# Two Flamingo layers on one core: the gate's rounding under the up projection, and weight splits put off behind the routing

## The chip, the cores and the metric

The kernel runs on one core of a Trainium2 chip. A core has TensorE (PE) for matrix products, VectorE (DVE), ScalarE (ACT), GpSimd (POOL) and SyncE (SP); each works through its own queue of instructions in order and waits on semaphores for the others. The metric is the device time of one execution in microseconds (us). The kernel before took 1800.84 us, the median of 3 runs (1798.96 to 1802.85).

## The reference

The input x has 16 sequences of 112 tokens (1792 tokens in all) and 256 features. Four residual blocks follow each other; `g` are learned gates.

```
x = x + tanh(g_xattn[0]) * attention_0(layernorm(x), ctx)      # 16 heads of 64, context of 375
x = x + tanh(g_ffn[0])   * feed_forward_0(layernorm(x))        # quantised, 256 -> 768 -> 256
x = x + tanh(g_xattn[1]) * attention_1(layernorm(x), ctx)      # 16 heads of 16
x = x + tanh(g_ffn[1])   * mixture(layernorm(x))               # shared expert + top 2 of 8, 256 -> 1024 -> 256
```

The two blocks that matter here are

```
# feed_forward_0; q(v) = clip(round(v / s), -32768, 32767) * s with s = max|v| / 32767 over the whole tensor
x = q(x); up = q(x @ W_up.T); gate = q(x @ W_gate.T)
sig = clip(round(sigmoid(gate) * 65536), 0, 65535) / 65536
gate = q(gate * sig); o = q(gate * up); return o @ W_down.T
# mixture
shared = relu(normed @ sw1 + sb1) @ sw2 + sb2
probs = sigmoid(flat @ router_w.T); scores, idx = top_k(probs, 2); w = scores / (sum(scores) + 1e-6)
routed = sum over the two experts of w * (relu(flat @ ew1 + eb1) @ ew2 + eb2)
```

Each `q` needs the largest absolute value of a whole tensor before any of it can be rounded. With a scale s, rounding is a multiplication by 1/s and a round to the nearest integer.

## The kernel before

The program is a sequence of phases, each a block with a barrier of all engines at its end: a setup, attention 0, a normalisation with the quantisation of the weights, `feed_forward0_phase` (L631), attention 1, the mixture's front `moe_front_phase` (L1312) and `routed_experts_phase` (L1864). Products in near-float32 precision are three float16 matmuls each (high by high, low by high, high by low, L291 to L293), so every operand is split: ACT rounds it to float16 (the high part) and DVE subtracts that from the value (the low part).

**Feed-forward 0.** The 1792 tokens are four groups (`NG`) of 448 columns (`GW`); the 768 hidden features are six slices (`OC0`) of 128. A job is one slice of one group of one projection. PE does, group by group, the six up jobs and then the six gate jobs, into six PSUM slots. ACT copies each job to `U` or `G` (L710), and DVE reduces six of them to their largest absolute value (L774). After the last group, POOL's all-reduce (L742) spreads the maximum over the partitions and DVE makes the scales (L787 to L795). Then six slices of 1792 columns pass through a pipeline. ACT rounds the gate by adding the constant MAGIC (L714), DVE subtracts it again (L798), ACT takes the sigmoid (L699) and rounds it in the same way (L701, L754), DVE multiplies (L755) and reduces (L757). POOL rounds U meanwhile (L747). The result's maximum gives the next scale (to L805), ACT rounds again (L722, L726), DVE multiplies gate and up (L809) and reduces (L812). The last maximum gives the output scale and the gate of the residual (to L819). The output is rounded and split in four groups of 2688 columns (six slices of 448: L731 and L734 on ACT, L823 on DVE), each released to PE as a whole. PE does one token row `t` of 16 after another (18 matmuls each), DVE adds each to the residual (L763).

**The mixture's front.** It does the shared expert for all tokens, decides the routing, and prepares the weights of all nine experts. The shared expert runs in 32 steps: four groups of four rows, eight slices of 128 hidden features each. In step `n` PE computes the slice's up projection (into `m_p1`, printed `m_p`), ACT applies bias and relu (L1604) and rounds to float16 (L1608), DVE subtracts (`low(n)`, L1667), and three steps later (`LAG`) PE multiplies into `m_p2` (L1560). After a group's last slice `add(g)`, four DVE operations on L1674, moves `m_p2` to `y`; only then can PE begin the next group's second products, and POOL adds `y` to the output in memory (L1461). `add(g)` waits for the store of the group before, since there is one `y`.

Between these stand two other streams. 36 weight chunks of 512 KB come by DMA into three stage buffers (SP, L1433), and each is split by ACT (L1592) and DVE (L1655); SP refills a buffer when DVE has split what it held. The table `CHUNKS` gives the step in which a chunk is split. The routing is a long run of small DVE operations that ends in masks: three of 1120 columns for the tiles (L1818 first, then L1822) and two of 2048 columns for the rows (L1825). PE multiplies them in step `FIND_AT` (the find, L1530), DVE makes row indices, and POOL gathers the first token tiles (L1457). Then POOL makes the bias of each tile of tokens (L1465, L1470).

The order of all work inside an engine is the order in which the code issues it; there is no planner. The lines that decide when PE goes on at a group's edge are

```
def add(g):
    dve.wait_ge(down_done, g * HC1 + HC1)
    wait(dve, stored, 16 * g)
    for i in range(TG):
        nc.vector.tensor_scalar(y[:, i, :], p2[0:S, i, 0:D], gate[:], None, ALU.mult).then_inc(added, 1)
```

## Time and profile before

| | |
|---|---|
| median of 3 runs | 1800.84 us (1798.96 to 1802.85) |
| profiled execution | 1801.27 us |
| its span | 1799.5 us |
| granted clock of TensorE, mean | 0.897 |
| PE busy | 1422.7 us (79%) |
| DVE busy | 1245.4 us (69%) |
| ACT busy | 1138.1 us (63%) |
| POOL busy | 244.2 us (14%) |

The span runs from the first to the last instruction of one profiled execution; the execution's time is 1.8 us longer. Busy shares are means over phases with different limits. In the profile PE's "clock" is the granted share of full speed. A row of a timeline gives an instruction's start in us from the span's start, its length, engine, line and operation, what it writes and reads with the shapes, how many such follow each other (x4), and in brackets the idle time before it with what ended that. Names there have lost their numbers: `f0_G` is `f_G`, and `m_p1` and `m_p2` are both `m_p`. What the program calls `x_res` in the front is the large tensor `x_all`, in which masks and gathered tiles lie too.

### The profile page before, as it was taken

The numbers are of one execution on the slowest core, as the hardware profiler recorded it, in microseconds if no ns is written. First come the engines' busy times: TensorE is split into PE (matmuls) and PEld (weight loads), VectorE is DVE, ScalarE is ACT, GpSimd is POOL, SyncE is SP. The second block draws the span as 40 slices with busy tenths as digits, with TensorE's granted clock in tenths as the row PEclk, the third lists the DMA queues.
The fourth block names the chain that finished last, engine by engine and source line by source line (L and its number), as shares of the span: only waits on it lengthen the run. The fifth ranks groups of instructions, "written<-read, shape, count | busy, mean of one in ns | idle before, by whom it ended". The sixth has DMA issues, their size and how long they took to land. (4 is left out here: it accounts for less than half of the span.)

```text
span 1799.5 us, 40814 instructions
## 1 busy us (share of the span) xinstructions
PE 1422.7 (79%) x15436; PEld 1013.3 (56%) x15436; DVE 1245.4 (69%) x3030; ACT 1138.1 (63%) x2422; POOL 244.2 (14%) x202
## 2 busy tenths in 40 slices
PE   1799999999999954900738889898898476779996
PEld 1566676766766643500725666666665354558885
DVE  6567777777677777478447889888887676534443
ACT  5466666666666633465436888888887444546664
POOL 4400001000010013020050000000000004024443
PEclk9999999999999986955857999999998687879998
DMA  4110000100010010000010001011000424522222
GB/s 145 35 36 19 19 19 19 36 19 19 19 27 18 2 54 1 0 0 0 10 42 22 24 25 31 17 31 32 17 26 4 127 64 130 175 42 44 46 46 28
DMA packets 36652, 66.09 MB, mean 37 GB/s; under 512 B 5161, under 2 KB 25618, under 8 KB 36466
## 3 DMA queue, kind: packets, MB, share of 16 engines
q1 hardware_dynamic: 27890, 53.40, 9.7%
q0 software_dynamic: 8576, 10.10, 3.6%
q8 instruction: 129, 2.11, 0.5%
q14 instruction: 57, 0.47, 0.1%
HBM read 48.16 MB, written 16.24 MB: 36 GB/s over the span
## 5 line engine op out<-in xcount | busy, mean ns | idle before, releaser
L519 ACT ACTIVATE a_pt<-a_ps_t 125x336 f16<-125x336 f32 x256 | 102.6, 448 | 107.5 <-PE a_ps_t L450 107.2
L1180 ACT ACTIVATE a_p<-a_s,a_nb 112x375 f32<-112x375 f32 x256 | 140.9, 598 | 26.9 <-DVE a_nb L1281 26.0
L291 PE MATMUL a_ps_o<-a_vh,a_pt 125*128 125x64 f16 (+1 forms) x1536 | 153.2, 183 | 3.0 <-ACT a_pt L1193 0.8
L293 PE MATMUL a_ps_o<-a_vh,a_pt 125*128 125x64 f16 (+1 forms) x1536 | 151.3, 182 | 0.0
L292 PE MATMUL a_ps_o<-a_vl,a_pt 125*128 125x64 f16 (+1 forms) x1536 | 151.2, 182 | 0.0
L1105 PE MATMUL a_ps_t<-ident,a_p 112*128 112x112 f32 x768 | 119.4, 287 | 39.8 <-ACT a_p L1180 39.3
L511 ACT ACTIVATE a_p<-a_ps_s,a_nb 112x375 f32<-112x375 f32 x256 | 144.1, 573 | 3.0 <-DVE a_scaled L591 3.0
L291 PEld LDWEIGHTS a_ps_o<-a_vh,a_pt 125*128 125x128 f16 x1536 | 133.8, 98 | 15.7 <-ACT a_pt L1193 7.5
L292 PEld LDWEIGHTS a_ps_o<-a_vl,a_pt 125*128 125x128 f16 x1536 | 131.2, 98 | 11.2
L1272 DVE TENSOR_TENSOR a_s<-a_ps_s,a_mask 112x750 f32<-112x750 f32 x128 | 119.8, 936 | 25.4 <-PE a_ps_s L1095 20.4
L1105 PEld LDWEIGHTS a_ps_t<-ident,a_p 112*128 112x128 f32 x768 | 81.2, 148 | 95.1 <-issue 80.2
L1281 DVE CUSTOM_DVE_ANT_0 a_s<-a_s,a_fill 112x375 f32<-112x375 f32 x256 | 130.0, 546 | 5.5
L591 DVE TENSOR_SCALAR_CACHE_REDUCE a_scaled<-a_ps_s 112x375 f32<-112x375 f32 x256 | 129.0, 541 | 5.1 <-POOL x_res L544 3.9
L572 DVE TENSOR_TENSOR a_vl<-a_ps_j,a_vh 125x512 f16<-125x512 f32 x96 | 66.4, 692 | 93.2 <-ACT a_vh L495 93.2
L1966 ACT ACTIVATE e_h<-e_p,tile_b 128x128 f32<-128x128 f32 x280 | 86.8, 368 | 68.6 <-PE e_p L293 65.6
L293 PEld LDWEIGHTS a_ps_o<-a_vh,a_pt 125*128 125x128 f16 x1536 | 129.4, 97 | 0.0
L1998 DVE TENSOR_TENSOR e_hl<-e_h,e_hh 128x512 f16<-128x512 f32 x70 | 48.5, 692 | 101.8 <-ACT e_hh L1973 101.8
L597 DVE TENSOR_TENSOR a_pt<-a_ps_t,a_pt 125x336 f16<-125x336 f32 x256 | 116.9, 498 | 1.1 <-ACT a_pt L519 1.0
L291 PE MATMUL a_ps_j<-a_cx,a_wk 128*128 128x375 f16 x320 | 106.2, 332 | 14.0 <-POOL a_neg L1217 10.4
L291 PE MATMUL a_ps_j<-a_wv,a_cx 128*125 128x512 f16 (+1 forms) x384 | 111.2, 308 | 2.6 <-DVE a_kl L1233 1.3
L291 PE MATMUL e_p<-e_xth,w1h 128*128 128x128 f16 x560 | 110.3, 222 | 1.6 <-DVE e_xtl L1992 1.6
L292 PE MATMUL e_p<-e_xtl,w1h 128*128 128x128 f16 x560 | 110.2, 222 | 0.0
(366 smaller groups left out, 4656.4 us busy)
## 6 DMA issues: line engine op xcount, KB each, us to landing
m_stage<-in_w SPq DMA_DIRECT2D x36, 512.0 KB, 4.2
a_ctx<-in_ctxT SPq DMA_DIRECT2D x16, 375.0 KB, 3.6
ctx<-a_cx SPq DMA_DIRECT2D x16, 375.0 KB, 4.3
a_cx<-ctx SPq DMA_DIRECT2D x16, 375.0 KB, 3.7
a_mask<-in_mask SPq DMA_DIRECT2D x16, 164.1 KB, 2.3
x_res<-in_x SPq DMA_DIRECT2D x1, 1792.0 KB, 9.5
out_x<-x_res SPq DMA_DIRECT2D x16, 112.0 KB, 2.2
normed_rows<-x_res SPq DMA_DIRECT2D x4, 448.0 KB, 5.1
```

The lines of the kernel that those rows point to most:

```text
L291: nc.tensor.matmul(out, wh, mh, start=(i == 0), stop=False)
L292: nc.tensor.matmul(out, wh, ml, start=False, stop=False)
L293: last = nc.tensor.matmul(out, wl, mh, start=False, stop=(i == n - 1))
L511: nc.scalar.activation(p32[:, g % 2, i, 0:NC], ps_s[0:S, i, 0:NC], ACT.Exp, bias=nb[:, g % 2, i:i + 1], scale=SC, accum_out=rsum[:, h:h + ...
L519: nc.scalar.activation(pt[:, g % 2, i, 0, :, 0:S], ps_t[0:KV, i, 0:NKV * S].rearrange("p (t s) -> p t s", t=NKV), ACT.Copy).then_inc(pt_hi, 1)
L591: nc.vector.tensor_scalar(scaled[:, i, :], ps_s[0:S, i, 0:NC], -SC, None, ALU.mult, ALU.min, accum_out=nb[:, g % 2, i:i + 1]).then_inc(max ...
L597: nc.vector.tensor_tensor(pt[:, g % 2, i, 1, :, 0:S], ps_t[0:KV, i, 0:NKV * S].rearrange("p (t s) -> p t s", t=NKV), pt[:, g % 2, i, 0, :, ...
L1105: mm = nc.tensor.matmul(ps_t[:, 2 * (g % 2) + i, t * S:(t + 1) * S], p32[:, g % 2, i, t * KV:t * KV + 128], ident32[0:S, 0:S], start=(t == ...
L1180: nc.scalar.activation(p32[:, g % 2, i, 0:NC], s2[:, g % 2, i, :], ACT.Exp, bias=nb[:, g % 2, i:i + 1], scale=-1.0).then_inc(exp_done, 1)
L1272: nc.vector.tensor_tensor(s1[:, r], ps_s[0:S, :, 0:NC], maskt[:, b % 2:b % 2 + 1, :].to_broadcast([S, 2, NC]), ALU.mult).then_inc(masked, 1)
L1281: nc.vector.tensor_tensor_reduce(out=s2[:, r, i, :], in0=s1[:, r, i, :], in1=fill[:, r, i, :], scale=-SC, scalar=3.0e38, op0=ALU.add, op1= ...
L1966: nc.scalar.activation(h32[:, 2 * (i % 2) + c, (j % 4) * 128:(j % 4 + 1) * 128], p1[:, 2 * (i % 2) + c, (j % 4) * 128:(j % 4 + 1) * 128], ...
```

## The change

In the feed-forward PE does the 24 gate jobs first and then the 24 up jobs. The maximum, scale, rounding, sigmoid and gated product of the gate start when the gate jobs are done, and ACT alternates one take of an up job with one rounding or sigmoid, after four takes of lead (`AHEAD`). Rounding is now the conversion to int16 (or uint16 for the sigmoid) that a write of that type does; additions and subtractions of MAGIC are gone, and so is POOL's part. The output goes in eight groups of two rows (1344 columns): ACT rounds, DVE copies to float16 and subtracts. There are four all-reduces instead of three.

In the front, chunks 4 to 31 are split in other steps: none before step 10, one a step from 10 to 20, then two in every odd and one in every even step. The masks of tiles and rows are made in steps 10 to 13 and the find is in step 14. The tile bias is made by DVE in steps 18 to 25, a multiplication of 280 columns and a reduction to 35 for each slice. There are two `y` and two semaphores for stores, so `add(g)` waits for the store of group g - 2. POOL's first store is issued before the gathers, and SP's wait for the stores is now a wait of POOL's in the routed phase.

```diff
@@ feed_forward0_phase: PE and ACT @@
-            def group(g):
-                for j in range(NJ):
-                    w, o = (wup, wgt)[j // OC0], j % OC0
...
+            for n in range(2 * NJ):
+                m, g, o = job(n)
+                w = (wgt, wup)[m]
+                wait(pe, copied, n - 5)
...
+            def round_gate(o):
+                if o == 0:
+                    act.wait_ge(scal, 1)
+                nc.scalar.activation(g_int[:, o, :], G[:, o, :], ACT.Copy, scale=sc[:, 2:3]).then_inc(g_rounded, 1)
...
+            for n in range(NJ + AHEAD):
+                take(n)
+            extra = [(f, o) for o in range(OC0) for f in (round_gate, sigmoid)]
+            for n in range(NJ + AHEAD, 2 * NJ):
+                take(n)
+                if extra:
+                    f, o = extra.pop(0)
+                    f(o)
...
-                    for o in range(OC0):
-                        nc.gpsimd.tensor_scalar(U[:, o, :], U[:, o, :], sc[:, 1:2], MAGIC, ALU.mult, ALU.add
-                                                ).then_inc(u_rounded, 1)
@@ feed_forward0_phase: DVE @@
+            def gated_product(o):
+                dve.wait_ge(sig_raw, o + 1)
+                nc.vector.tensor_scalar(sig_int[:, o % 2, :], sig[:, o % 2, :], UQ, UQ - 1.0, ALU.mult, ALU.min
+                                        ).then_inc(sig_rounded, 1)
+                dve.wait_ge(sig_rounded, o + 1)
+                nc.vector.tensor_tensor(G[:, o, :], sig_int[:, o % 2, :], g_int[:, o, :], ALU.mult).then_inc(gated, 1)
...
-                nc.vector.scalar_tensor_tensor(out=ol[:, g, :, :], in0=G[:, :, cc], scalar=-MAGIC,
-                                               in1=oh[:, g, :, :], op0=ALU.add, op1=ALU.subtract
-                                               ).then_inc(o_split, 1)
+                rounded = u_int[:, :, g * W2:(g + 1) * W2]
+                dve.wait_ge(o_rounded, g + 1)
+                nc.vector.tensor_copy(oh[:, g], rounded).then_inc(o_hi, 1)
                 dve.wait_ge(o_hi, g + 1)
+                nc.vector.tensor_tensor(ol[:, g], rounded, oh[:, g], ALU.subtract).then_inc(o_split, 1)
@@ moe_front_phase @@
-        RANK_AT, MOVE_AT, FIND_AT, COUNTED = 5, 8, 12, 15
-        CHUNKS = {4: [4], 6: [5], 8: [6], STEPS: [29], STEPS + 1: [30], STEPS + 2: [31], STEPS + 3: [32, 33]}
-        CHUNKS.update({n: [n - 3] for n in range(10, STEPS)})
+        RANK_AT, MOVE_AT, FIND_AT, COUNTED = 5, 8, 14, 15
+        CHUNKS = {n: [n - 6] for n in range(10, 21)}
+        CHUNKS.update({n: [(3 * n) // 2 - 16 + i for i in range(1 + n % 2)] for n in range(21, STEPS)})
+        CHUNKS.update({STEPS + 2: [32], STEPS + 3: [33]})
...
-            sp.wait_ge(stored, 16 * NG)
...
-            nc.gpsimd.tensor_tensor(bsel, tile_hot[:].unsqueeze(2).to_broadcast([128, MAXT, HC1, E]),
...
-                wait(dve, stored, 16 * g)
+                wait(dve, stored[g % 2], 16 * (g // 2))
...
+                if n == 10:
+                    place_tile(1, part16[:, 0])
+                    place_tile(2, part16[:, 1])
                 if n == 11:
+                    place_tile(0, token[:])
+                if n in (12, 13):
+                    place_row(n - 12)
...
+                j = n - FIND_AT - 4
+                if 0 <= j < HC1:
+                    bias(nc.vector.tensor_tensor(bsel, tile_hot[:],
+                                                 b1[:, 0:E, j].unsqueeze(1).to_broadcast([128, MAXT, E]), ALU.mult))
+                    bias(nc.vector.tensor_reduce(tile_b1[:, :, j], bsel, AX.X, ALU.add))
@@ routed_experts_phase: POOL, after its first gathers @@
+            for landed in stored:
+                pool.wait_ge(landed, 16 * (NG // 2))
```

DVE in the feed-forward, before, from the end of the scales on (`f_sc` holds the scales, `f_sig` the sigmoid, `f_omx` the maxima):

```order
L790 TENSOR_TENSOR f_sc<-f_sc 128x1
L795 TENSOR_SCALAR f_sc<-f_sc 128x1
L798 TENSOR_SCALAR f_G<-f_G 128x1792 x2
L754 TENSOR_SCALAR f_sig<-f_sig 128x1792
L755 TENSOR_TENSOR f_G<-f_sig,f_G 128x1792
L757 TENSOR_REDUCE f_omx<-f_G 128x1
L798 TENSOR_SCALAR f_G<-f_G 128x1792
L754 TENSOR_SCALAR f_sig<-f_sig 128x1792
L755 TENSOR_TENSOR f_G<-f_sig,f_G 128x1792
```

The same place after, from the end of the gate's scales on (`f_si` and `f_gi` are the 16-bit integers of sigmoid and gate, `f_gmx` the maxima of the projections):

```order
L795 TENSOR_SCALAR f_sc<-f_sc 128x1
L750 TENSOR_REDUCE f_gmx<-f_U 128x1
L766 TENSOR_SCALAR f_si<-f_sig 128x1792
L769 TENSOR_TENSOR f_G<-f_si,f_gi 128x1792
L771 TENSOR_REDUCE f_omx<-f_G 128x1
L766 TENSOR_SCALAR f_si<-f_sig 128x1792
L769 TENSOR_TENSOR f_G<-f_si,f_gi 128x1792
L771 TENSOR_REDUCE f_omx<-f_G 128x1
L750 TENSOR_REDUCE f_gmx<-f_U 128x1
L766 TENSOR_SCALAR f_si<-f_sig 128x1792
L769 TENSOR_TENSOR f_G<-f_si,f_gi 128x1792
L771 TENSOR_REDUCE f_omx<-f_G 128x1
```

Maxima of `f_U` now stand between the gated products of the gate, and each product reads the two integer tensors; the rounding of `f_G` (L798) is gone from DVE.

DVE in the front, before, from step 9's `low` to `add(0)` (`x_res` holds the masks; L1655 is the low half of a chunk):

```order
L1667 TENSOR_TENSOR m_hl<-m_h,m_hh 128x448
L1818 TENSOR_TENSOR x_res<-m_num_t,m_pos_tile 112x32x35
L1822 TENSOR_TENSOR x_res<-x_res,m_part 112x32x35 x2
L1822 TENSOR_TENSOR x_res<-x_res,m_token 112x32x35
L1825 TENSOR_TENSOR x_res<-m_lane,m_pos_row 112x2048 x2
L1667 TENSOR_TENSOR m_hl<-m_h,m_hh 128x448
L1655 SCALAR_TENSOR_TENSOR w<-m_stage,w 128x4x256
L1667 TENSOR_TENSOR m_hl<-m_h,m_hh 128x448
L1655 SCALAR_TENSOR_TENSOR w1l<-m_stage,m_nws,w1h 128x1024
L1674 TENSOR_SCALAR m_y<-m_p,m_gate 112x256 x4
```

The same place after, where L1662 is `low`, L1650 a chunk's split, L1669 `add`, and L1810, L1815 and L1819 are the masks:

```order
L1810 TENSOR_TENSOR x_res<-m_num_t,m_pos_tile 112x32x35
L1662 TENSOR_TENSOR m_hl<-m_h,m_hh 128x448
L1650 SCALAR_TENSOR_TENSOR w1l<-m_stage,m_nws,w1h 128x1024
L1815 TENSOR_TENSOR x_res<-x_res,m_part 112x32x35 x2
L1662 TENSOR_TENSOR m_hl<-m_h,m_hh 128x448
L1650 SCALAR_TENSOR_TENSOR w1l<-m_stage,m_nws,w1h 128x1024
L1669 TENSOR_SCALAR m_y<-m_p,m_gate 112x256 x4
L1815 TENSOR_TENSOR x_res<-x_res,m_token 112x32x35
L1662 TENSOR_TENSOR m_hl<-m_h,m_hh 128x448
L1650 SCALAR_TENSOR_TENSOR w<-m_stage,w 128x4x256
L1819 TENSOR_TENSOR x_res<-m_lane,m_pos_row 112x2048
L1662 TENSOR_TENSOR m_hl<-m_h,m_hh 128x448
```

The third tile mask (the second L1815 row) and both row masks (L1819, of which the first is the last row here) stand behind `add(0)`; two tile masks and two splits still stand ahead of it.

POOL in the front, before, from the gathers on:

```order
L1457 DMA x_res<-normed_rows,tile_pick 128x256 x3
L1465 TENSOR_TENSOR x_res<-m_tile_hot,m_b 128x2240
L1470 TENSOR_TENSOR x_res<-x_res 128x280x4
L1470 TENSOR_TENSOR x_res<-x_res 128x280x2
L1470 TENSOR_TENSOR tile_b<-x_res 128x280
L1461 DMA out_x<-m_y 112x4x256 x4
```

And after, from its first store on (`x_res` in a store is the second `y`):

```order
L1459 DMA out_x<-m_y 112x4x256
L1466 DMA x_res<-normed_rows,tile_pick 128x256 x3
L1459 DMA out_x<-x_res 112x4x256
L1459 DMA out_x<-m_y 112x4x256
L1459 DMA out_x<-x_res 112x4x256
```

The four multiplications and additions have left POOL, and the first store stands ahead of the gathers.

## Rows read from the trace of the kernel before

**Rows 1.** The page, its first row.

```profile
span 1799.5 us, 40814 instructions
```

**Rows 2.** Windows of the feed-forward; columns as its first row says.

```profile
core 0: us, PE busy (x) PEld busy (x) DVE busy (x) ACT busy (x) POOL busy (x), PEclk, DMA share, GB/s
...
772.50:820.90 48.40, 0.00 (x0) 0.00 (x0) 41.33 (x26) 33.38 (x19) 13.02 (x6) 0.50 0.00 0
...
862.00:897.00 35.00, 34.40 (x288) 33.72 (x288) 16.16 (x19) 12.17 (x5) 0.00 (x0) 0.93 0.00 1
```

**Rows 3.** Timeline of DVE in the feed-forward: start, length, operation, idle before.

```profile
766.95 2.95 DVE L774 TENSOR_REDUCE f_gmx<-f_G  x1 [3.83 <-ACT f_G L710]
...
772.38 0.15 DVE L795 TENSOR_SCALAR f_sc<-f_sc 128x1 f32<-128x1 f32 x1
774.48 1.09 DVE L798 TENSOR_SCALAR f_G<-f_G 128x1792 f32<-128x1792 f32 x1 [1.95 <-ACT f_G L714]
...
827.88 2.03 DVE L809 SCALAR_TENSOR_TENSOR f_G<-f_U,f_G 128x1792 f32<-128x1792 f32 x1 [5.40 <-ACT f_G L726]
...
851.92 0.16 DVE L815 TENSOR_REDUCE f_mx<-f_omx 128x1 f32<-128x6 f32 x1
...
853.59 0.15 DVE L819 COPY f_sc<-f_sc 128x1 f32<-128x1 f32 x1
859.01 2.96 DVE L823 SCALAR_TENSOR_TENSOR f_ol<-f_G,f_oh 128x2688 f16<-128x2688 f32 x1 [5.26 <-ACT f_oh L734]
```

**Rows 4.** Timeline of ACT in the feed-forward.

```profile
712.92 0.54 ACT L710 ACTIVATE f_U<-f_pj 128x448 f32 x1 [2.21 <-PE f_pj L293]
...
766.25 0.54 ACT L710 ACTIVATE f_G<-f_pj 128x448 f32 x1 [0.59 <-PE f_pj L293]
...
776.24 1.28 ACT L699 ACT_TABLE_LOAD   x1
...
779.35 1.79 ACT L701 ACTIVATE f_sig<-f_sig,f_mc 128x1792 f32<-128x1792 f32 x1
...
839.87 3.45 ACT L726 ACTIVATE f_G<-f_G,f_mneg 128x1792 f32<-128x1792 f32 x2
```

**Rows 5.** Windows of the mixture's front, columns as in the windows above.

```profile
1474.60:1499.80 25.20, 25.15 (x188) 19.07 (x188) 17.71 (x24) 15.50 (x21) 11.23 (x5) 0.93 0.37 119
1499.80:1517.90 18.10, 0.15 (x1) 0.00 (x0) 10.16 (x10) 2.25 (x3) 6.32 (x4) 0.56 0.55 141
1517.90:1542.00 24.10, 24.07 (x156) 17.66 (x156) 12.16 (x14) 15.49 (x21) 1.20 (x1) 0.91 0.55 149
1542.00:1547.40 5.40, 0.19 (x2) 0.00 (x0) 4.46 (x7) 2.25 (x3) 0.00 (x0) 0.89 0.38 116
1547.40:1582.80 35.40, 20.20 (x132) 15.80 (x132) 17.84 (x19) 16.48 (x19) 2.34 (x2) 0.74 0.60 158
```

**Rows 6.** Timeline of DVE in the mixture's front.

```profile
1461.42 2.56 DVE L1822 TENSOR_TENSOR x_res<-x_res,m_part 112x1120 f16<-112x1120 f16 x2
...
1465.14 4.49 DVE L1825 TENSOR_TENSOR x_res<-m_lane,m_pos_row 112x2048 f16<-112x2048 f16 x2
1469.54 0.62 DVE L1667 TENSOR_TENSOR m_hl<-m_h,m_hh 128x448 f16<-128x448 f32 x1
1470.07 1.22 DVE L1655 SCALAR_TENSOR_TENSOR w<-m_stage,w 128x1024 f16<-128x1024 f32 x1
...
1492.61 6.84 DVE L1655 SCALAR_TENSOR_TENSOR w1l<-m_stage,m_nws,w1h 128x1024 f16<-128x1024 f32 x1 [0.41 <-ACT w1h L1592]
...
1516.21 1.66 DVE L1674 TENSOR_SCALAR m_y<-m_p,m_gate 112x256 f32<-112x256 f32 x4 [7.91 <-DMA out_x<-m_y]
...
1574.94 1.65 DVE L1674 TENSOR_SCALAR m_y<-m_p,m_gate 112x256 f32<-112x256 f32 x4
```

**Rows 7.** Timeline of POOL in the mixture's front.

```profile
1492.41 5.95 POOL L1465 TENSOR_TENSOR x_res<-m_tile_hot,m_b 128x2240 f32<-128x2240 f32 x1
```

**Rows 8.** Timeline of ACT at the end of the front.

```profile
1566.37 1.06 ACT L1592 ACTIVATE w<-m_stage 128x1024 f16<-128x1024 f32 x1 [2.60 <-DMA m_stage<-in_w]
...
1577.22 1.06 ACT L1592 ACTIVATE w<-m_stage 128x1024 f16<-128x1024 f32 x1 [0.44 <-DMA m_stage<-in_w]
```

More of the change, by code:

```diff
@@ L692, in _ @@
[L692 to L702 removed]
+                     wdn[:, 0, o, :], wdn[:, 1, o, :]) for o in range(OC0)]).then_inc(down_done, 1)
@@ L728, in _, with take @@
-            act.wait_ge(scal, 3)
-            for g in range(NG):
-                cc = slice(g * GW, (g + 1) * GW)
-                nc.scalar.activation(G[:, :, cc], G[:, :, cc], ACT.Identity, bias=m_c[:], scale=sc[:, 7:8]
-                                     ).then_inc(o_rounded, 1)
-                act.wait_ge(o_rounded, g + 1)
-                nc.scalar.activation(oh[:, g, :, :], G[:, :, cc], ACT.Identity, bias=m_neg[:]).then_inc(o_hi, 1)
+            def take(n):
+                m, g, o = job(n)
+                act.wait_ge(job_done, n + 1)
+                nc.scalar.activation((G, U)[m][:, o, g * GW:(g + 1) * GW], pj[:, n % 6, 0:GW], ACT.Copy
+                                     ).then_inc(copied, 1)
@@ new lines, in _ @@
+            for n in range(NJ + AHEAD):
[6 more added lines that the diff above has]
+                    f(o)
+            for f, o in extra:
+                f(o)
+            act.wait_ge(scal, 2)
+            for o in range(OC0):
+                nc.scalar.activation(u_int[:, o, :], U[:, o, :], ACT.Copy, scale=sc[:, 1:2]).then_inc(u_rounded, 1)
@@ L814, in _ @@
[L814 to L821 removed]
+                product(o)
@@ L1453, in _, with add_shared @@
             pool.wait_ge(rows_out, 16 * NG)
+            def add_shared(g):
+                pool.wait_ge(added, TG * (g + 1))
+                nc.gpsimd.dma_start(out[g * TG:(g + 1) * TG].rearrange("t p d -> p t d"), y[g % 2], accum_op=ALU.add
+                                    ).then_inc(stored[g % 2], 16)
+            add_shared(0)
             pool.wait_ge(index_ready, 1)
```

267 lines of the change are left out of this document (117 added, 150 removed).

## The prediction

> **What bounds the kernel now.** I read three views, in this order: the page's span, the windows of the two phases that the change touches, and in them the timelines of VectorE (DVE), ScalarE (ACT) and GpSimd (POOL). The span is 1799.5 us [rows 1]. Nothing outside `feed_forward0_phase` and `moe_front_phase` is edited but a wait of POOL's in the routed phase, so the question is how much earlier each of the two reaches its closing barrier.
>
> In the feed-forward TensorE (PE) projects until about 767, then does nothing while the rounding runs (0.00 between 772.5 and 820.9, where DVE is busy 41.3 of 48.4 us), and works again from 862.0 for 35 us with the down projection [rows 2]. The reader should see three serial links between: the gate's rounding, sigmoid and gated product (scale ready at 772.53, end of DVE's window near 821), the second product (827.88 to 851.92), and the split of the output (first half at 859.01) [rows 3]. DVE is the steady resource of the first two.
>
> In the front PE keeps pace with DVE and ACT inside a group of eight steps and stops between groups: 18.1 us before group 2 and 5.4 before group 3 [rows 5]. Each stop ends when DVE's four `L1674` operations have emptied the PSUM tile `m_p2`. The first stop is that long because DVE's `L1674` waited 7.91 us for the store of the previous `m_y`, and because DVE was slowed before it: a split that takes 1.27 took 6.84 at 1492.61, exactly when POOL began the 5.95 us tile bias [rows 6, 7].
>
> **Feed-forward, step by step.** All 24 gate jobs come first. ACT takes one job every (766.25 - 712.92) / 47 = 1.135 us [rows 4], so the last gate job is taken at 712.92 + 23 x 1.135 + 0.54 = 739.6 and the reduction of 2.95 [rows 3] ends at 742.5, not 769.9. The scale chain took 772.53 - 769.90 = 2.6; it has four small operations of 0.2 fewer, so the gate's scale is ready at 744.3, 28.2 earlier.
>
> From there ACT does two things: 20 more takes of 0.545, six roundings and six sigmoids. Two roundings in a row take 3.45 [rows 4], so 1.7 each, and the table load is 1.28: 10.9 + 20.4 + 1.3 = 32.6, to about 777. The up projection therefore ends ten us later than now, with PE waiting for ACT. This costs nothing, because DVE is later still. DVE's list from 744.3 on: four reductions of the up projection, 4 x 2.95 = 11.8; six gated products, each a conversion (priced by L798, 1.09), a product and a reduction (2.03 each, as L809's row), with hand-overs 5.2, so 31.2; and the two scale chains with their all-reduces, 3.1. That is 46.1. It first waits 3.3 for the sixth up job behind ACT's first rounding and 1.2 for the first sigmoid. The scale of the gated product is ready at 744.3 + 4.5 + 46.1 = 794.9. The up projection's own scale is ready at 787.7, so ACT rounds six slices of U until 787.7 + 6 x 1.7 = 797.9 and then one slice of the gated product, to 799.7. There DVE's first product starts; before, it started at 827.88. ACT, not DVE, ends that wait. Six products with their reductions take the 24.0 us they take now (827.88 to 851.92 [rows 3]), since DVE is the pace and ACT's roundings of 1.7 hide under its 4.0. The output's scale is ready at 799.7 + 24.0 + 1.8 = 825.6 instead of 853.7 (the same 1.8 behind 851.92): 28.1 gained. The old rounding subtractions that leave (six L701 and six L726 on ACT, L798 on DVE, L747 on POOL) are worth only what of this they make possible.
>
> Last the output split. Before, the first down matmul came 8.3 us behind the scale: 5.3 in two operations on ACT, 2.96 on DVE, all on 2688 columns [rows 3]. Now a group has 1344: ACT 5.3/4 = 1.3, DVE's copy 1344/1792 x 1.09 = 0.8, the subtraction 1344/1792 x 2.03 = 1.5, and hand-overs of 0.3, 3.9 in all. That gains 4.4. Behind it DVE needs 0.8 + 1.5 and two additions of (16.16 - 3 x 2.96) / 16 = 0.46 [rows 2], 3.2 us for two token rows, and PE 35/8 = 4.4, so PE sets the rate and its 35 us stay [rows 2]. **Feed-forward: -28.1 - 4.4 = -32.5.**
>
> None of the integer-typed operations is in the trace. Upper price: if a conversion of float32 to 16 bit runs like a two-source operation (2.03 instead of 1.09 [rows 3]), the six conversions add 5.6, part of it in the 4.5 of waits, and the copy and subtraction 0.7: gain 27.5. Lower: the output pieces at half my price, and the waits gone, 2.5 more: gain 35. I take the middle because L798 is the nearest row (one source, both ends in SBUF, float32).
>
> Here a rule matters. The row shows 1.09 us for 1792 columns from one source against 2.03 with two [rows 3]. The Trainium skill, "VectorE: DVE Perf Modes", section "What auto-detection actually checks", gives the reason for the factor of two and goes further: a one-source operation whose tensors are all 16 bit runs four columns a cycle, a two-source one with all three at 16 bit runs two, and one with a float32 output stays at one. By that rule the integer copy and the subtraction of the split would take an estimated 0.5 and 0.9 instead of 0.8 and 1.5, the products would stay at 2.03, and the sum would be 1756. No row of before shows a 16-bit one-source operation.
>
> **Front, step by step.** Group 1 resumes at 1474.6 [rows 5], when `add(0)` is done. Two things leave DVE's queue ahead of it: three splits of about 1.25 (chunks 4 to 6) and, moved behind it, one tile placement (1.28) and both row placements (4.49) [rows 6]. Together they are 9.5 us of work; ahead of them DVE also waits for ACT's hidden activations, which come no earlier, so I count 2.4 of the first and 4.3 of the second: resume at 1468.0, -6.7.
>
> Group 2: from there before's 25.2 us to the end of its last up job (1474.6 to 1499.8 [rows 5]), plus 3.6 for the find: it now stands in step 14 and waits for the second row placement, since from step 12's low half to the find DVE has two low halves (0.53, the distance of 1469.54 and 1470.07), two splits (1.2) and both row placements (2.24 each), 7.9, against 5.1 us of PE in two steps (156 matmuls in 24.07 us are 8.7 steps of 18, at a clock of 0.91: 2.5 a step at the full one [rows 5]), and 0.8 of hand-overs; plus an estimated 1.5 for a step and a half of PE at the slower level after that stop. That gives 1498.3. The stop behind it is then the ordinary one of 5.4 [rows 5]: y has two buffers, so `add(1)` waits for no store, and POOL multiplies nothing. Resume at 1503.7 against 1517.9, -14.2. What hides the removed store wait is the second buffer; without it 7.9 would return.
>
> Group 3: before, 29.5 us later (1517.9 to 1547.4). In steps 21 to 27 two steps bring three splits and two pieces of bias to DVE: 2 x 0.53 + 3 x 1.2 + 2 x 0.95 = 6.6 us, where PE needs 5.1. The 0.95 is an estimate for two operations of 280 columns: 0.15 for one column [rows 3] and 2.03 for 1792 give 0.45 each. ACT, with three splits of 1.06 [rows 8] and two pairs of activations, is also near PE. Three such pairs and a bit cost 1.5 each, 4.8 in all: resume at 1538.0, -9.4. So part of the gain is given back here, as splits that were put off.
>
> End: before, DVE's last `L1674` at 1574.94 [rows 6] came 27.5 behind the resume, with nine chunks to split. At the tail six chunks start within 1577.22 - 1566.37 = 10.85 [rows 8], 2.17 each: the chunks' arrival through three stage buffers, not an engine, is the pace. Now eight chunks stand between the resume and `add(3)`: 27.5 - 2.3 = 25.2, so 1563.2, **-11.7**. The phase ends at 1582.8 [rows 5], 6.2 behind the last `L1674`, with the landing of POOL's last store, issued right behind `add(3)`. SP's wait for that store is removed, but POOL's own drain at the barrier follows the same store, so I count nothing; if only SP's wait held the barrier, up to 4.5 more go (two end splits remain in any case). The wait added to POOL in the routed phase stands behind its first gathers, for stores long landed.
>
> **Sum.** The profiled execution took 1801.27 us, its span and 1.8 around it, 0.4 above the median of the runs shown. 1801.27 - 32.5 - 11.7 = 1757.1; I predict 1757.
>
> **Rivals.** Least gain at the front: three chunks in two steps asks for one per 1.7 us, faster than the 2.17 at which chunks arrived at the tail. If arrival binds from step 21 on, or a landing takes longer once the gathers and stores share the queues, the putting off of chunks is paid back: with half of the 18 chunks exposed at 1 us more each, the front gains 3: 1766. For it: the tail rows [rows 8]. Against: from step 21 to `add(3)` 18 chunks at 2.17 need 39, and the walk above gives them 58.
>
> Integer operations dear on DVE (27.5 instead of 32.5): 1762. For it: no row shows one. Against: L798's 1.09.
>
> A better front: the find's wait hidden and steps 21 to 27 at PE's pace give 16.5: 1752. For it: in the 24.1 us of group 2 DVE is busy only 12.16 and ACT 15.49 [rows 5]. Against: the count of 6.6 against 5.1.
>
> Slower than before: the gated product and the second product read integers in two operands. DVE's path holds 12 products of 2.03 and 6 conversions of 1.09, 31 us, and 8 pairs of split operations of 2.3. If every integer form took 2.5 times its float32 row, the first would add 46; the pairs would take 5.8 + 1.0, more than PE's 4.4, and add 8 x 2.4 = 19 and 3.5 ahead of the first: 1757 + 69 = 1826. It decides from a factor of about 2. Nothing in the profile speaks for it. A milder one of the same kind: a table load at every change between sigmoid and copy on ACT, 11 x 1.28 = 14 us, ending near DVE's list; before, ACT returned to Identity at 779.35 with no load in between [rows 4], which speaks against it.
>
> **Chances.** Forecast as walked (1753 to 1760) 0.54, weak front 0.12, dear integers 0.14, better front 0.15, slower 0.03, and 0.02 that gains and losses cancel or nearly. I leave the extremes out and take 1745 to 1773. A change of 0.2% (3.6 us) is about what a measurement of this kernel can tell from none: faster 0.95, same 0.01, slower 0.04.
>
> **What would show it.** Right: in the profile of after, the reduction of the last gate group starts near 739.6, DVE is busy over 90% between 750 and 795, the first product starts near 800 and the first down matmul near 829.6. The front is then shifted by 32.5: PE resumes groups 1, 2 and 3 at 1435.5, 1471.2 and 1505.5, and the last add starts at 1530.7. Wrong: conversions from float32 of 1792 columns at 2 us; products above 2.1 us; ACT table loads between the sigmoids; ACT idle for `m_stage` in steps 21 to 27; or a store wait that returns at `add(2)`. The prediction as a whole falls if the feed-forward gains less than 25 us, since the front cannot make that good.

## The result, and the profile after

| | before | after |
|---|---|---|
| median | 1801.13 us (4 runs, 1798.96 to 1802.85) | 1751.72 us (4 runs, 1748.40 to 1754.55) |
| ratio | | 0.9726, 95% interval 0.9703 to 0.9749 |
| profiled execution | 1801.27 us | 1748.40 us |
| span | 1799.5 us | 1746.7 us |

The change makes the kernel 49.4 us faster; 1757 had been predicted, with a range of 1745 to 1773. In a second set of five runs on another chip the changed kernel took 1751.51 us (1750.75 to 1756.46), 49.3 less than before there.

The two profiles differ by 52.8 us. Each phase's length, from marks that both traces have (PE's first projection, DVE's first normalisation instruction behind the feed-forward, POOL's first memsets of attention 1 and of the front, its first gather of the routed phase):

| phase | before | after | difference | predicted |
|---|---|---|---|---|
| before the feed-forward's first job | 711.49 | 712.35 | +0.9 | 0 |
| feed-forward | 185.80 | 149.34 | -36.5 | -32.5 |
| normalisation behind it | 24.06 | 22.98 | -1.1 | 0 |
| attention 1 | 477.05 | 471.75 | -5.3 | 0 |
| mixture's front | 189.06 | 178.18 | -10.9 | -11.7 |
| routed experts, to the end | 212.04 | 212.10 | +0.1 | 0 |

The feed-forward in the windows of the changed kernel (start and end, length, busy time of PE, PE's weight loads, DVE, ACT and POOL, then granted clock, DMA share, GB/s). The first window is the up projection with the rounding under it, the second the rest of the rounding, the last the down projection; they answer to [rows 2]:

```profile
core 0: us, PE busy (x) PEld busy (x) DVE busy (x) ACT busy (x) POOL busy (x), PEclk, DMA share, GB/s
...
740.00:774.50 34.50, 26.95 (x136) 12.41 (x135) 29.24 (x22) 30.76 (x34) 0.38 (x1) 1.00 0.00 0
774.50:824.00 49.50, 1.60 (x9) 0.61 (x7) 42.55 (x35) 22.43 (x17) 1.81 (x3) 0.55 0.00 0
827.70:861.70 34.00, 33.06 (x288) 32.81 (x288) 16.69 (x32) 7.63 (x6) 0.00 (x0) 0.96 0.01 1
```

PE, DVE and ACT are all busy for 27 to 31 of the 34.5 us under the up projection; PE gives way to ACT there, as forecast. DVE's timeline, the rows that answer to [rows 3]:

```profile
740.36 2.95 DVE L750 TENSOR_REDUCE f_gmx<-f_G 128x1 f32<-128x2688 f32 x1 [3.86 <-ACT f_G L701]
...
744.90 0.15 DVE L795 TENSOR_SCALAR f_sc<-f_sc 128x1 f32<-128x1 f32 x1
748.14 2.95 DVE L750 TENSOR_REDUCE f_gmx<-f_U 128x1 f32<-128x2688 f32 x1 [3.09 <-ACT f_U L701]
751.24 1.09 DVE L766 TENSOR_SCALAR f_si<-f_sig 128x1792 uint16<-128x1792 f32 x1
752.37 2.02 DVE L769 TENSOR_TENSOR f_G<-f_si,f_gi 128x1792 f32<-128x1792 uint16 x1
...
793.71 0.16 DVE L814 TENSOR_TENSOR f_sc<-f_sc 128x1 f32<-128x1 f32 x1
799.00 2.03 DVE L777 TENSOR_TENSOR f_G<-f_ui,f_gi 128x1792 f32<-128x1792 int16 x1 [5.13 <-ACT f_gi L730]
...
826.29 0.51 DVE L827 CAST f_U<-f_ui 128x1344 f16<-128x1344 int16 x1 [1.55 <-ACT f_ui L734]
826.84 0.86 DVE L829 TENSOR_TENSOR f_U<-f_ui,f_U 128x1344 f16<-128x1344 int16 x1
```

The product of two integer tensors takes 2.02 and 2.03, as its float32 form did, and the conversion to uint16 1.09. What ends DVE's wait at 799.00 is ACT's rounding, which came late for this reason:

```profile
748.13 1.28 ACT L712 ACT_TABLE_LOAD   x1
...
773.08 3.60 ACT L701 ACTIVATE f_U<-f_pj 128x448 f32<-128x448 f32 x8
787.11 10.18 ACT L727 ACTIVATE f_ui<-f_U,f_sc 128x1792 int16<-128x1792 f32 x6 [10.43 <-DVE f_sc L762]
797.20 10.17 ACT L730 ACTIVATE f_gi<-f_G,f_sc 128x1792 int16<-128x1792 f32 x6
```

There is one table load. ACT stands idle for 10.43 us in front of the up projection's scale, which DVE makes behind a gated product. The six roundings take 10.2 us, 1.7 each.

PE's waits for DVE in the front of the changed kernel, three group edges and the find, in order of time (L1555 is the first second-layer product of a group, L1525 the find):

```profile
1426.15 0.68 PE L1555 MATMUL m_p<-w,m_hh 128*112 128x256 f16 x2 [5.26 <-DVE m_y L1669]
...
1440.82 0.96 PE L1525 MATMUL m_px<-x_res 112*128 112x105 f16 x16 [2.46 <-DVE x_res L1819]
...
1461.99 0.68 PE L1555 MATMUL m_p<-w,m_hh 128*112 128x256 f16 x2 [5.26 <-DVE x_res L1669]
...
1497.37 0.67 PE L1555 MATMUL m_p<-w,m_hh 128*112 128x256 f16 x2 [10.97 <-DVE m_y L1669]
```

The 18.1 us stop before group 2 [rows 5] is the ordinary 5.26 now, and the ordinary 5.4 before group 3 has become 10.97. The windows around it:

```profile
1462.00:1486.00 24.00, 23.61 (x155) 17.50 (x156) 18.11 (x25) 15.25 (x20) 1.33 (x1) 0.93 0.64 178
1486.00:1497.00 11.00, 0.40 (x3) 0.00 (x0) 9.65 (x13) 6.55 (x9) 0.00 (x0) 0.66 0.65 201
```

PE ran through group 2's steps in 24.0 us, as before, and then waited for what DVE still had to do: 9.65 us of it in 11.0. ACT did wait for chunks here, eight times between 1473.8 and 1493.3, 5.7 us in all, which the prediction had named as a sign against itself. But DVE was busy for 27.1 of the 29.6 us from 1467.75 to PE's resume and waited only 2.0 for ACT, so the chunks' arrival is the smaller part of this stop. Near the end ACT waits for chunks again, and longer, answering to [rows 8]:

```profile
1515.38 1.06 ACT L1587 ACTIVATE w<-m_stage 128x1024 f16<-128x1024 f32 x1 [1.59 <-DMA m_stage<-in_w]
1517.09 1.15 ACT L1587 ACTIVATE w1h<-m_stage,m_nws 128x1024 f16<-128x1024 f32 x1 [0.66 <-DMA m_stage<-in_w]
1519.61 1.15 ACT L1587 ACTIVATE w1h<-m_stage,m_nws 128x1024 f16<-128x1024 f32 x1 [1.37 <-DMA m_stage<-in_w]
1522.35 1.06 ACT L1587 ACTIVATE w<-m_stage 128x1024 f16<-128x1024 f32 x1 [1.58 <-DMA m_stage<-in_w]
```

### The profile page after: what moved, and what is told of

Its sections match the earlier page's. It is cut to its first block and busy times, and to the rows that moved or that the text cites. A ratio compares the mean times of both kernels' runs of the same rounds, so it can differ in the third digit from the quotient of the medians.

```text
span 1746.7 us, 40641 instructions
## 1 busy us (share of the span) xinstructions
PE 1418.8 (81%) x15436; PEld 1009.3 (58%) x15436; DVE 1231.2 (70%) x3050; ACT 1112.9 (64%) x2416; POOL 220.5 (13%) x193
## 3 DMA queue, kind: packets, MB, share of 16 engines
q1 hardware_dynamic: 27890, 53.40, 10.2%
## 5 line engine op out<-in xcount | busy, mean ns | idle before, releaser
L1276 DVE TENSOR_TENSOR a_s<-a_ps_s,a_mask 112x750 f32<-112x750 f32 x128 | 119.8, 936 | 21.1 <-PE a_ps_s L1099 16.3
```

Of the source, the lines that this page charges most:

```text
L1276: nc.vector.tensor_tensor(s1[:, r], ps_s[0:S, :, 0:NC], maskt[:, b % 2:b % 2 + 1, :].to_broadcast([S, 2, NC]), ALU.mult).then_inc(masked, 1)
```

## The experiments

Twelve experiments ran (eleven other kernels, and the changed one again), in three sets on three chips, each beside runs of the kernel before on its chip; ratios are to those. Phase lengths are from each run's one profile, by the marks of the table above.

| run | median us | ratio (95%) | feed-forward | attention 1 | front |
|---|---|---|---|---|---|
| before | | | 185.80 | 477.05 | 189.06 |
| after | 1751.72 | 0.9726 (0.9703 to 0.9749) | 149.34 | 471.75 | 178.18 |
| e1 feed-forward alone | 1763.48 | 0.9804 (0.9787 to 0.9820) | 150.62 | 474.00 | 189.35 |
| e2 front alone | 1788.92 | 0.9938 (0.9919 to 0.9956) | 185.88 | 474.12 | 181.38 |
| e3 up scale early | 1751.60 | 0.9730 (0.9713 to 0.9746) | 148.14 | 476.06 | 180.86 |
| e4 add first | 1740.08 | 0.9667 (0.9651 to 0.9683) | 149.25 | 476.40 | 166.09 |
| e5 one y | 1755.18 | 0.9732 (0.9704 to 0.9760) | 149.45 | 477.28 | 181.39 |
| e6 bias on POOL | 1757.81 | 0.9762 (0.9738 to 0.9785) | 149.74 | 472.06 | 186.75 |
| e7 old chunk table | 1751.79 | 0.9720 (0.9697 to 0.9742) | 150.65 | 475.84 | 180.07 |
| e8 output in four | 1755.28 | 0.9744 (0.9710 to 0.9778) | 151.91 | 476.56 | 178.95 |
| e9 after again | 1751.51 | 0.9739 (0.9720 to 0.9758) | 149.30 | 471.61 | 180.04 |
| e10 e3 and e4 | 1738.31 | 0.9657 (0.9641 to 0.9673) | 147.89 | 473.99 | 168.19 |
| e11 e10, old table | 1739.74 | 0.9662 (0.9643 to 0.9681) | 148.11 | 473.35 | 168.95 |
| e12 e10, find later | 1735.16 | 0.9640 (0.9622 to 0.9658) | 147.91 | 474.01 | 165.02 |

### e1 and e2: the two parts alone

e1 is the kernel before with the changed feed-forward function; e2 is the changed kernel with the old one.

```diff
# e1: before.py, with feed_forward0_phase and AHEAD of the changed kernel
# e2: the changed kernel, with feed_forward0_phase of before.py
```

> The kernel before with the changed feed-forward alone; the front is the old one. Theory (the parts add up): the feed-forward phase shortens by the 36 us that the profile of the changed kernel shows for it, and the front keeps its old length, so about 1801 - 36 = 1765, up to 3 less if attention 1 keeps part of its shortening. Rival 1 (attention 1's 5 to 6 us come from the feed-forward change, as its clock rises earlier after a shorter pause): 1759, and every profile with the new feed-forward shows attention 1 near 461 us. Rival 2 (those us are chance of the clock): attention 1 scatters between 461 and 467 whichever feed-forward is used.

> The changed front with the old feed-forward. Theory: the front gives the 10.9 us that the profile of the changed kernel shows, so about 1790, with PE resuming group 1, 2 and 3 about 6.6, 14 and 8 us earlier, counted from the front's own start. Rival 1: attention 1 stays at 466.5 us here, since its shortening belongs to the feed-forward change. Rival 2: it scatters.

e1 gained 36.8 us, e2 11.4 (by the intervals of the ratios 32 to 38 and 8 to 15 us). Their sum is 48.2, the whole change 49.4: the parts add up. The feed-forward phase is 35.2 shorter in e1 and the front 7.7 shorter in e2. Attention 1 took 474.0 and 474.1 us, with the new and with the old feed-forward, so its 5.3 us in the first comparison are not an effect of the feed-forward: the rival of chance stands. (The expectations count attention 1 from a later mark, POOL's first addition, 10.55 us behind the one used here: their 466.5 is the 477.05 of before.) Both expected totals (1765 and 1790) were close. The walk inside e2's front was not: PE resumed groups 1, 2 and 3 at 73.2, 107.8 and 144.8 us of the front, 3.0, 11.7 and 4.2 earlier than before, where 6.6, 14 and 8 were expected.

### e9: the changed kernel again

> The changed kernel once more, beside the versions of the same call. It answers how far attention 1, which nothing in the change touches, scatters: it was 471.8 us in the profile of the changed kernel and 472.1 to 477.3 in seven others, with the old and the new feed-forward alike. Theory (that profile caught a short one): 1751 to 1754, attention 1 nearer 475. Rival (it belongs to this kernel): 472 again.

Attention 1 took 471.6 again in the profile, so the expectation of 475 missed. But the five executions of this one kernel lie between 1750.75 and 1756.46 us, with mean clocks of 0.908 to 0.916, and over all profiles attention 1 lies between 471.6 and 477.3 with nothing in it changed. What goes with its length is how long TensorE was granted the lower of its two clocks in it. Added up from windows of 5 us, that is an estimated 81 us in the two profiles of the changed kernel (471.75 and 471.61 us long), 100 in e5's (477.28) and 103 before (477.05). A part of this is when the clock first rises. Windows of the same stretch, 38.7 to 48.7 us behind POOL's first memset of the phase, before and after:

```profile
960.00:970.00 10.00, 9.49 (x84) 5.61 (x84) 5.49 (x16) 6.74 (x13) 0.00 (x0) 0.53 0.00 0
```

```profile
923.40:933.40 10.00, 8.15 (x122) 5.68 (x120) 8.18 (x23) 9.16 (x19) 0.00 (x0) 1.00 0.01 2
```

PE is still at 1.2 GHz in the first (granted 0.53) and at 2.4 GHz in the second (1.00), and does 84 matmuls against 122. The first rise is not all of it: e5's came 35 us into the phase, as in the changed kernel, and its attention 1 is still 5.5 us longer, with more time at the lower clock further on. Why the clock is lower for longer in one execution was not settled. For a comparison of versions it is scatter of some 5 us.

### e3: the up projection's scale ahead of gated product 4

```diff
             largest_of_all(UP)
-            gated_product(4)
             dve.wait_ge(mx_all, 2)
             scale_of(am[:, UP:UP + 1], sc[:, 0:1], sc[:, 4:5], sc[:, 1:2]).then_inc(scal, 1)
+            gated_product(4)
```

> The changed kernel with DVE's scale chain of the up projection moved ahead of gated product 4. In the changed kernel ACT stood idle 10.4 us for that scale and the first product of gate and up waited 5.1 us for ACT. Theory (ACT's six roundings of the up projection are on the path): the scale comes 4.5 us earlier (782.3 instead of 787.1), less 0.6 for the all-reduce that is no longer covered. ACT's roundings end before the gated scale is ready, and the first product starts about 1.8 us behind that scale: 796.2 instead of 799.0. So 2.5 to 3 us faster in the feed-forward, about 1749. Rival (the wait is DVE's own, for the gated scale): no change beyond the 0.6 added.

Inside the rounding it did what was expected. DVE's first product of gate and up, with what it waited for:

```profile
796.95 2.02 DVE L777 TENSOR_TENSOR f_G<-f_ui,f_gi 128x1792 f32<-128x1792 int16 x1 [1.85 <-ACT f_gi L730]
```

The wait fell from 5.13 to 1.85, and the first down matmul came 112.69 us into the phase instead of 115.40, 2.7 earlier. The phase as a whole was only 1.2 shorter, because the down projection took 35.5 us instead of 33.9. All four profiles with this edit (e3, e10, e11, e12) show 35.2 to 35.5 there, and of the eight with the new feed-forward without it six show 33.9 to 34.4 and two 35.2. The medians (1751.60 against 1751.72) can't tell so little. So the scale's lateness was on the path, its worth in the whole phase is 1.2 to 1.4 (149.3 to 147.9 in e10), and whether the later rise of the clock belongs to the edit is open.

### e4: add(g) ahead of low(n) and the splits

```diff
+                if n % HC1 == LAG and n > LAG:
+                    add(n // HC1 - 1)
                 if n < STEPS:
                     low(n)
                 for c in CHUNKS.get(n, ()):
                     split(c)
-                if n % HC1 == LAG and n > LAG:
-                    add(n // HC1 - 1)
```

> The changed kernel with DVE's add(g) ahead of low(n) and the splits of the same step, n = 11, 19, 27, 35. The stop of PE at a group's edge was 5.3 us twice and 11 us once. Theory (the stop is DVE's order, not the add itself: the add waits behind low(n), which waits for ACT, which waits for PE's up job of that step): the stops fall to 1 to 2 us, PE resumes group 1 about 4 earlier, group 2 about 7, and the end of the front gains 5 to 9 us, the rest lost to the arrival of chunks at 2.2 us each: about 1745. Rival (chunks are the pace of the whole second half): the stops shrink and PE then waits for splits elsewhere; add(3) moves by less than 2 us, 1751.

1740.08 us, 11.6 less than the changed kernel and 11.5 less than e3 on the same chip (ratios to before 0.9667 against 0.9726), and more than expected. The front is 166.1 us long, against 179.9 in the mean of the five profiles with the whole new front (after, e2, e3, e8, e9). PE's rows at the three edges in e4:

```profile
1428.91 0.68 PE L1555 MATMUL m_p<-w,m_hh 128*112 128x256 f16 x2 [2.93 <-DVE m_y L1669]
...
1461.35 0.43 PE L1555 MATMUL m_p<-w,m_hh 128*112 128x256 f16 x2 [1.87 <-DVE x_res L1669]
...
1490.97 0.67 PE L1555 MATMUL m_p<-w,m_hh 128*112 128x256 f16 x2 [6.24 <-DVE m_y L1669]
```

The stops are 2.93, 1.87 and 6.24 instead of 5.26, 5.26 and 10.97; 1 to 2 had been expected of all three. The "ordinary" stop of 5.3 us, which the prediction took as given, was DVE's order: the add, whose input PE had finished a step before, stood behind a `low` that waits for ACT and so for PE, and behind a split. The edit moves it ahead of both, so their shares were not taken apart.

### e5: one y

```diff
-                wait(dve, stored[g % 2], 16 * (g // 2))
+                wait(dve, stored[0], 16 * g)
...
-                    nc.vector.tensor_scalar(y[g % 2][:, i, :], p2[0:S, i, 0:D], gate[:], None, ALU.mult).then_inc(added, 1)
+                    nc.vector.tensor_scalar(y[0][:, i, :], p2[0:S, i, 0:D], gate[:], None, ALU.mult).then_inc(added, 1)
```

> The changed kernel with one y again (add(g) waits for the store of group g - 1), all else changed. POOL's store of group 0 was issued at 70.4 us of the front, and add(1) began at 103.9: if the landing takes the 5.7 to 11 us of before, it is down by 82, so theory 1 (the second y buys nothing once the first store is issued ahead of the gathers; the 7.9 us wait of before came from the store's place behind POOL's bias) expects 1751 and stops of PE as in the changed kernel, 5.3, 5.3 and 11. Theory 2, the prediction's own (the second buffer hides the 7.9): stop before group 2 of about 13 and a kernel 5 to 8 us slower, 1758.

PE's stops are those of the changed kernel, and none waits for a store:

```profile
1436.41 0.67 PE L1555 MATMUL m_p<-w,m_hh 128*112 128x256 f16 x2 [5.26 <-DVE m_y L1669]
...
1470.81 0.68 PE L1555 MATMUL m_p<-w,m_hh 128*112 128x256 f16 x2 [5.26 <-DVE m_y L1669]
...
1507.11 0.68 PE L1555 MATMUL m_p<-w,m_hh 128*112 128x256 f16 x2 [10.96 <-DVE m_y L1669]
```

The front is 181.4 us, at the upper end of the 178.2 to 181.4 of the five profiles with the whole new front. The prediction's own theory fell: the 7.9 us wait of before is gone without the second buffer. What removed it is that POOL issues group 0's store earlier: 106.5 us into the front before, behind the gathers and the tile bias, and 75.0 in e5, 32 us ahead of `add(1)`. Whether the new place ahead of the gathers or the bias off POOL would have been enough alone no run shows. The median of 1755.18 lies above, its interval (0.9704 to 0.9760) spans the changed kernel's, and attention 1 was 477.3 in that profile.

### e6: the tile bias back on POOL

```diff
+            pool.wait_ge(tile_hot_ready, 1)
+            nc.gpsimd.tensor_tensor(bsel, tile_hot[:].unsqueeze(2).to_broadcast([128, MAXT, HC1, E]),
...
             for g in range(1, NG):
                 add_shared(g)
...
-                j = n - FIND_AT - 4
-                if 0 <= j < HC1:
```

> The changed kernel with the tile bias back on POOL (behind the gathers, ahead of the store of group 1), none on DVE in steps 18 to 25. Theory 1: POOL's 17 us of work slow DVE by its lock as before (a split took 6.84 instead of 1.27): about 9 us of DVE lost in steps 17 to 19, but 8 x 1.1 us of bias leave DVE, and the store of group 1 is issued about 6 us late, which y's second buffer hides. Group 2 resumes 6 to 9 later, group 3 about as late as in the changed kernel: 1750 to 1756. Rival (DVE's bias is what stretches the stop before group 3 from 5.3 to 11): that stop falls by 4 to 5 and the kernel is faster, 1747.

1757.81 us, 1.8 above the range expected, and the front 186.75, 6.9 longer than the mean of those five profiles (179.9). POOL's and DVE's rows at the place:

```profile
1455.89 5.89 POOL L1470 TENSOR_TENSOR x_res<-m_tile_hot,m_b 128x2240 f32<-128x2240 f32 x1
```

```profile
1455.50 7.38 DVE L1660 SCALAR_TENSOR_TENSOR w<-m_stage,w 128x1024 f16<-128x1024 f32 x1
1462.80 2.53 DVE L1867 TENSOR_TENSOR m_digit<-m_digit,m_tile_ex 1x35 f32<-1x35 f32 x1
```

A split of 1.22 takes 7.38 while POOL multiplies, and an operation on 35 numbers 2.53 instead of 0.18. With two more behind them DVE loses some 9.7 us at this one place; POOL's work is 11.5 us in all, not the 17 of the expectation. The same bias on DVE is eight pieces of 1.1, 8.8 us, spread over eight steps. PE's stop before group 2 is 12.69, and the one before group 3 still 10.49, with no bias on DVE: the rival, that the bias stretches that stop, fell.

### e7: the old table of chunks

```diff
-        CHUNKS = {n: [n - 6] for n in range(10, 21)}
-        CHUNKS.update({n: [(3 * n) // 2 - 16 + i for i in range(1 + n % 2)] for n in range(21, STEPS)})
-        CHUNKS.update({STEPS + 2: [32], STEPS + 3: [33]})
+        CHUNKS = {4: [4], 6: [5], 8: [6], STEPS: [29], STEPS + 1: [30], STEPS + 2: [31], STEPS + 3: [32, 33]}
+        CHUNKS.update({n: [n - 3] for n in range(10, STEPS)})
```

> The changed kernel with the old table of chunks (4, 5 and 6 split inside the routing chain, one a step from 10 on), all else changed. Theory 1 (my walk): three splits return to the chain and cost 2.4 us at the resume of group 1, but steps 21 to 27 keep PE's pace, so the stop before group 3 is 5.3 and not 11, and the tail has the same chunks: equal or up to 4 us faster than the changed kernel, 1748 to 1752. Rival (putting off chunks is what made the front faster): slower by 3 or more, 1755.

The stop before group 3 is the ordinary one again:

```profile
1500.20 0.67 PE L1554 MATMUL m_p<-w,m_hh 128*112 128x256 f16 x2 [5.26 <-DVE m_y L1668]
```

and the front is 180.07 us long, the kernel 1751.79: no difference. Group 3 resumes 139.6 us into the front instead of 141.0, but the end comes 40.5 behind it instead of 37.2. Putting off three chunks buys nothing and costs nothing; it moves the same wait from the tail to the edge.

### e8: the output in four groups

```diff
-    NP2, W2 = B // 2, 2 * S
+    NP2, W2 = NG, GW
```

> The changed kernel with the feed-forward's output split in four groups of four token rows (2688 columns) instead of eight of two. In the changed kernel the first down matmul came 3.0 us behind the scale: 1.36 on ACT, 0.51 (copy) and 0.86 (subtraction) on DVE for 1344 columns. Theory (durations grow with the columns): 2.6 + 1.0 + 1.6 = 5.2, so the first matmul is 2.2 later; PE's 34 us stay: 1754. Rival (PE's later groups wait for the larger pieces too): 3 to 5 us slower.

The first group on DVE:

```profile
827.03 0.86 DVE L827 CAST f_U<-f_ui 128x2688 f16<-128x2688 int16 x1 [2.67 <-ACT f_ui L734]
827.93 1.56 DVE L829 TENSOR_TENSOR f_U<-f_ui,f_U 128x2688 f16<-128x2688 int16 x1
```

The first down matmul came 117.56 us into the phase, 2.2 later, as expected, and the phase is 2.6 longer; the interval of the time holds the changed kernel. The two sizes give the rates: (0.86 - 0.51) / 1344 = 0.26 ns a column for the copy from int16 to float16, and (1.56 - 0.86) / 1344 = 0.52 ns for the subtraction with three 16-bit tensors, against 1.09 / 1792 = 0.61 (fixed part included) for a conversion from float32.

### e10, e11 and e12: versions on top

e10 has the edits of e3 and e4. e11 adds the old table to it, e12 the find one step later:

```diff
-        RANK_AT, MOVE_AT, FIND_AT, COUNTED = 5, 8, 14, 15
+        RANK_AT, MOVE_AT, FIND_AT, COUNTED = 5, 8, 15, 15
```

> Both improvements on the changed kernel: the up projection's scale ahead of gated product 4, and add(g) ahead of low(n). Theory (the 2.7 us that the first brought inside the feed-forward's rounding are real and were lost in the scatter of attention 1): 12 us of e4 plus 2.7: 1737. Rival (they are given back by a later rise of the clock in the down projection, which was 1.5 us longer in that profile): 1739 to 1740.

> e10 with the old table of chunks. With add first, a stop of 6.2 us was left before group 3; the old table removed the long one (11 to 5.3) in the changed kernel without gain at the end, since more chunks then stood behind it. Theory 1 (the end of the front is set by how early the chunks are asked for, and they can be asked for earlier with this table in groups 1 and 2): 3 to 5 us faster than e10, 1733. Theory 2 (given back at the tail again): equal to e10 within 2.

> e10 with the find in step 15 instead of 14 (and all that follows it one step later). PE waited 2.2 to 2.6 us for the second row mask there. Theory (the wait is hidden by one more step of PE, 2.5 us): it vanishes, and with it the 1.2 us of slower clock behind it: 2 to 3 us faster than e10 if DVE does not bind in steps 19 to 26. Rival (DVE binds from there, since the bias moves one step later into the double splits): no change.

e10 took 1738.31, between what its two theories said, and doesn't decide between them. e11 (1739.74) equals it: given back at the tail again. e12 took 1735.16, 3.2 less than e10, and is the fastest (the two intervals overlap a little): 16.3 us below the changed kernel on the same chip and 3.6% below before (0.9622 to 0.9658). PE no longer waits for the find, and its stops are

```profile
1425.39 0.68 PE L1555 MATMUL m_p<-w,m_hh 128*112 128x256 f16 x2 [2.93 <-DVE m_y L1669]
...
1453.91 0.43 PE L1555 MATMUL m_p<-w,m_hh 128*112 128x256 f16 x2 [1.97 <-DVE x_res L1669]
...
1486.18 0.68 PE L1555 MATMUL m_p<-w,m_hh 128*112 128x256 f16 x2 [8.28 <-DVE m_y L1669]
```

so part of the gain comes back in the last one, 8.28 instead of e10's 6.89.

## Why the prediction was right, and where it missed

**Gate first, rounding under the up projection.** Counted from PE's first job, the gate's scale was due at 32.8 and came at 32.7; the gated scale at 83.4 and 81.5; the first product at 88.2 and 86.65; the output's scale at 114.1 and 112.4. The mechanism held link by link, and what ended the wait at the first product was ACT, as said. The 1.9 us at the gated scale were two small terms: DVE waited 3.75 (3.09 and 0.66) where 4.5 was counted, and its work was 1.0 shorter, half of it since the all-reduce of the up projection (0.55) lay under a gated product. e3 showed that the order of two DVE pieces left another 2.7 us there.

**Integer operations.** Products and conversions cost what their float32 rows did, the value taken. The output pieces were too dear in the sum: 0.8 + 1.5 was counted and 0.51 + 0.86 measured, so the first matmul came 3.0 behind the scale instead of 3.9. These numbers had been worked out beside the sum, 0.5 and 0.9, from the Trainium skill, "VectorE: DVE Perf Modes", section "What auto-detection actually checks". e8's two sizes agree with its factors of four and two: 0.26 and 0.52 ns a column, against (2.02 - 0.16) / 1791 = 1.04 for the products with a float32 output. Here the rule was the better guide than scaling a float32 row.

**The down projection.** "Its 35 us stay" missed by 1.3: from the first matmul to the next phase it took 33.9 instead of 35.3. PE's rows where the length of a matmul falls, before and after:

```profile
862.02 0.46 PE L291 MATMUL f_po<-f_wdn,f_oh 128*112 128x256 f16 x1 [95.89 <-DVE f_ol L823]
...
866.97 0.28 PE L293 MATMUL f_po<-f_wdn,f_ol 128*112 128x256 f16 x1
```

```profile
827.75 0.46 PE L293 MATMUL f_po<-f_wdn,f_U 128*112 128x256 f16 x1 [51.65 <-DVE f_U L829]
...
830.73 0.27 PE L295 MATMUL f_po<-f_wdn,f_U 128*112 128x256 f16 x1
```

The clock rose 4.9 us behind the first matmul before and 3.0 behind it after. With e1 and e7 at 35.2 for the same code this is scatter. So of the 4.0 us by which the feed-forward did better than 32.5, 1.7 had come up to the output's scale, 1.0 came with the output pieces, and 1.3 with the clock.

**The front.** -11.7 was predicted, -10.9 shown in the first profile and -9.3 in the mean of the five with the whole new front (178.18, 181.38, 180.86, 178.95, 180.04). Set on before's axis by POOL's marks (42.0 us apart), group 1 resumed at 1468.1 (predicted 1468.0), group 2 at 1504.0 (1503.7), group 3 at 1539.4 (1538.0), and the last add began at 1564.0 (1563.2). That they agree to tenths is luck of this profile: in the other four, group 1 resumed 1.2 to 3.5 us later. The steps behind these were less good than their sum. The find's wait was 2.46, not 3.6. A step and a half of PE at half the clock would cost 3.8 by the prediction's own 2.5 a step, not the 1.5 that it took; the trace shows an estimated 1.7 (granted 0.72, 0.50 and 0.93 in three windows of 2 us from 1440.8 on), so that term's size held and its working did not. The loss by double splits came as a longer stop (10.97 instead of 5.26, 5.7 us) and not as slower steps, with 4.8 counted. And "what hides the removed store wait is the second buffer" was wrong: e5 took it away and nothing came back. Of group 2's earlier resume the larger part is the bias off POOL: with it back (e6) group 2 resumes 114.6 us into the front instead of 105.6 to 107.9, against 119.5 before, and 6.9 of the mean's 9.3 us are gone. The step that failed is the attribution, not the size: 7.9 us were put down to the second buffer, which is worth nothing here, and the ordinary stop of 5.4 was held fixed, of which e4 took back 2.3 and 3.4 us. That SP's removed wait is worth nothing held: from POOL's last store to its first gather of the routed phase it is 10.6 us before and 10.7 after.

**What was missing.** Attention 1 was 5.3 and the normalisation 1.1 shorter in the profile, which the sum held at nothing. The first is scatter of the clock (e1, e2, e9). The second, 22.3 to 23.0 in all profiles with the new feed-forward and 23.8 and 24.1 with the old, goes with the change. DVE there waits 0.83 instead of 1.78 us for ACT's square root, which stands between ACT's work on weights that arrive by DMA, but no run took it apart. The medians' gain, 49.4 against 44.2, is the feed-forward's 2.7 to 4.0 more, this 1 us, and clock, less the front's 1 to 2; the share of the clock is what is left over and was not measured by itself.

**The rivals.** Dear integers and the slow mixed form fell (2.02 and 2.03 us rows); so did repeated table loads (one). The weak front did not come in its size (3 us), but its mechanism is there in part: ACT waits for chunks in steps 21 to 27 and at the tail, and e7 and e11 give back at the tail what the old table wins at the edge. The chunks are not the only pace, since e4 made the front 13.8 us shorter with the same table; no run changed their arrival alone. The better front did not come with the change, but e4 shows that it was there, by another edit.

## What to carry to other kernels

Ask of each stop at an edge whether what is waited for stood behind something in its engine's queue that waits for the waiting engine: moving one four-instruction add ahead of such a wait gave some 11 us, as much as all the front's own changes. A reduction over a whole tensor is hidden by computing first the tensor whose maximum is needed first. Work on POOL is not free for DVE: 11.5 us of it cost DVE 9.7 in one place, more than the 8.8 that DVE needs to do it itself. A second buffer should be priced by the wait left once the queue order is right, which can be none.
